# Moving two scale operations of a tile from VectorE to ScalarE, and the second tile's statistics ahead of the first tile's

## The reference

```python
# part 1: a selective scan over l for 512 channels and 16 states, added through a tanh gate
u, dt, B, C = ...            # from ctx: projection, causal conv, silu, small projections
for l in range(512):
    state = state * exp(dt[l] * A) + (dt[l] * u[l]) * B[l]
    y[l] = (state * C[l]).sum(-1)
y = (y + D * u) * silu(layernorm(x))
x = x + tanh(g_xattn) * y.T
# part 2: a gated MLP with weights of -1, 0, 1 and activations rounded to 8 bit
def bitlinear(v, w):         # v: rows of 512 (gate, up) or 2048 (down)
    v = v * rsqrt(mean(v*v) + 1e-6)
    s = 127 / clip(max|v|, 1e-5)
    return round(clip(v*s, -128, 127)) / s  @  (round(clip(w*sw, -1, 1)) / sw).T
n = layernorm(x)
h = silu(bitlinear(n, w_gate)) * bitlinear(n, w_up)
x = x + tanh(g_ffn) * bitlinear(h, w_down)
```

## Time and profile before

| | us |
|---|---|
| median of 3 runs | 628.78 |
| lowest, highest | 627.72, 630.99 |
| profiled execution, own time | 626.36 |
| its span in the trace | 624.5 |
| mean granted TensorE clock of the profiled run, share of full speed | 0.969 |

### The profile page before, as it was taken

The page is one execution under the profiler, slowest core; times in us unless marked ns, Lnnn a source line. Parts: engine busy times, 40 slices in busy tenths (PEclk is TensorE's granted clock), DMA queues, the critical chain, the costliest instruction groups (busy, mean ns, idle before and its releaser), DMA issues. The chain is left out here.

```text
span 624.5 us, 9211 instructions
## 1 busy us (share of the span) xinstructions
PE 502.3 (80%) x3014; PEld 337.1 (54%) x3014; DVE 564.4 (90%) x777; ACT 511.4 (82%) x761; POOL 519.6 (83%) x286
## 2 busy tenths in 40 slices
PE   6999665866676788879777888888687978799997
PEld 2443354755574565656454655555455655555553
DVE  2899989999999999999998999999989999987564
ACT  4869799886997898969598989786889898778784
POOL 2568799999999999999999999999999999941000
PEclk9999768889889999999999999999999999999999
DMA  8992931710840010018301101075101110000001
GB/s 282 399 413 92 363 127 34 270 51 2 312 188 6 11 41 5 31 35 334 143 30 35 35 34 35 35 268 204 35 34 35 35 34 19 1 17 18 18 18 50
DMA packets 29985, 64.47 MB, mean 103 GB/s; under 512 B 3681, under 2 KB 11873, under 8 KB 26866
## 3 DMA queue, kind: packets, MB, share of 16 engines
q1 hardware_dynamic: 29938, 63.89, 28.2%
HBM read 55.75 MB, written 8.13 MB: 102 GB/s over the span
## 5 line engine op out<-in xcount | busy, mean ns | idle before, releaser
L755 POOL TENSOR_TENSOR area_s<-area_s,b_bc 128x1024 f32<-128x1024 f32 x128 | 300.7, 2368 | 10.0 <-DVE u_all L1318 5.7
L438 PE MATMUL pY<-ident,area_s 128*128 128x128 f32 x640 | 103.1, 287 | 79.2 <-DVE area_s L1326 76.3
L438 PEld LDWEIGHTS pY<-ident,area_s 128*128 128x128 f32 x640 | 73.2, 145 | 107.5 <-DVE area_s L1326 78.4
L1002 ACT ACTIVATE pA<-dt_all,a_neg 128x512 f32<-128x512 f32 x160 | 107.8, 682 | 19.2 <-DVE area_s L1318 13.8
L1318 DVE TENSOR_TENSOR_SCAN area_s<-pA,area_s 128x512 f32<-128x512 f32 x96 | 114.3, 1205 | 4.8 <-ACT pA L1002 4.8
L481 PE MATMUL pG<-wq_gu,area_f 128*128 128x512 fp8e4 x448 | 106.1, 379 | 4.9 <-ACT area_f L952 3.6
L747 POOL TENSOR_TENSOR u_all<-u_all 128x1024 f32<-128x1024 f32 x44 | 104.1, 2366 | 0.2 <-DMA u_all<-bc_rows 0.2
L1326 DVE TENSOR_TENSOR area_s<-area_s,pC 128x512 f32<-128x512 f32 x144 | 95.3, 664 | 1.6 <-DVE area_s L1318 0.9
L432 PE MATMUL pC<-ident,xdT 128*128 128x128 f32 x576 | 90.5, 284 | 3.8 <-DVE area_s L1326 2.6
L432 PEld LDWEIGHTS pC<-ident,xdT 128*128 128x128 f32 x576 | 69.6, 143 | 11.5 <-DVE area_s L1326 9.2
L481 PEld LDWEIGHTS pG<-wq_gu,area_f 128*128 128x128 bf16 x448 | 41.1, 98 | 52.3 <-ACT area_f L960 5.2
(11 more groups left out here) (197 smaller groups left out, 978.2 us busy)
## 6 DMA issues: line engine op xcount, KB each, us to landing
b_bc<-bc_rows SPq DMA_DIRECT2D x16, 1024.0 KB, 7.4
area_s<-x SPq DMA_DIRECT2D x32, 256.0 KB, 3.0
u_all<-bc_rows SPq DMA_DIRECT2D x14, 512.0 KB, 6.0
b_bc<-w_gate SPq DMA_DIRECT2D x1, 4096.0 KB, 15.2
...
```

The lines of the kernel that those rows point to most:

```text
L438: mm = pe.matmul(pY[:, k * P:(k + 1) * P], src[:, k * P:(k + 1) * P], ident[:, :], is_transpose=True, start=(first and k == 0), stop=(last ...
L755: gp.tensor_tensor(db[c % NDB], du[s % 2].rearrange("p (a l) -> p a l", a=1).to_broadcast([P, CH, L]), b_bc[:, CH * c:CH * c + CH, :], ALU ...
L1002: act.activation(exp_bank(s, n), dt_all[:, s, :], ACT.Exp, scale=a_neg[:, s % NT, n:n + 1]).then_inc(S["s_exp"], 1)
```

## The change

Five edits.

1. CS leaves `x_scales`: ScalarE computes it in `gate_scale`, right after `scale_x` (in the late part after `copy_xqT`). The semaphore f_xs now counts four per tile and CS has f_cs.
2. OSC leaves `h_scales`: ScalarE computes it in `out_scale`, after the second `scale_h` (before the `copy_hqT`s). f_hs now counts three per tile and OSC has f_osc.
3. In a first-tile step VectorE's `x_scales(t1)` moves from n = 7 to n = 6 (ahead of scan 7 and the product of state 6), GpSimd's `x_rstd(t1)` one `times_b` forward, ScalarE's `scale_x(t1)` from n = 8 to n = 7.
4. In a first-tile step ScalarE's `x_sum`, `centre` (n = 3) and `x_deviation` (n = 4) of the second tile move ahead of `centre` of the first one, to where they are in the other steps; the variance is now an operation of its own (`x_variance`), at n = 7 in a first-tile step.
5. `centre(t1)` stands ahead of `scale_h`, not behind it, at n = 5; `x_scales` of a unit's first tile waits for both centrings, since they count on one semaphore, and the squares of a unit's second tile go to its own buffer.

The core of the diff:

```diff
@@ GpSimd, step
                 times_b(s, NDB + 1)
-                times_b(s, NDB + 2)

                 if t1 % NT == 0:
                     x_rstd(t1)
+                times_b(s, NDB + 2)
@@ ScalarE
             def x_sum(t):

                 act.wait_ge(S["s_x1"], (t // NT) * NT + NT)
-                act.wait_ge(S["f_xn"], t)
+
+                past(act, S["f_xn"], t - (1 if (t - 1) % NT == 0 else 0))
                 past(act, S["f_xqp"], t - 1)
...
+            def gate_scale(t):
+                act.wait_ge(S["f_xs"], 4 * t + 2)
+                past(act, S["f_silu"], FC * t - FC)
+                act.activation(col(CS[t % 2]), col(M2), ACT.Copy, scale=k_gate[:, :]).then_inc(S["f_cs"], 1)
...
+            def out_scale(t):
+                act.wait_ge(S["f_hs"], 3 * t + 1)
+                past(act, S["f_o"], t - 1)
+                act.activation(col(OSC[t % 2]), col(M3), ACT.Copy, scale=k_out[:, :]).then_inc(S["f_osc"], 1)
@@ ScalarE, step
-                    if n == (2 if t1 % NT else 8):
+                    if n == (2 if t1 % NT else 7):
                         scale_x(t1)
-                    if n == 3 and t1 % NT and (t1 + 1) % NT:
+                        gate_scale(t1)
+                    if n == 3 and (t1 + 1) % NT:
                         x_sum(t1 + 1)
                         centre(t1 + 1)
-                    if n == 4 and t1 % NT and (t1 + 1) % NT:
+                    if n == 4 and (t1 + 1) % NT:
                         x_deviation(t1 + 1)
+                        if t1 % NT:
+                            x_variance(t1 + 1)
+                    if n == 5 and t1 % NT == 0:
+                        centre(t1)
                     if n == (4 if t1 % NT else 9):
                         copy_xqT(t1, pG[0][:, :])
                     if n in (5, 6) and t2 >= 0:
                         scale_h(t2, n - 5)
-                    if n == 5 and t1 % NT == 0:
-                        centre(t1)
+                        if n == 6:
+                            out_scale(t2)
+                    if n == 7 and t1 % NT == 0:
+                        x_variance(t1 + 1)
...
-                    if n == 9 and t1 % NT == 0:
-                        x_sum(t1 + 1)
-                    if n == 10 and t1 % NT == 0:
-                        centre(t1 + 1)
-                        x_deviation(t1 + 1)
@@ ScalarE, late part
                 scale_h(t - 1, 1)
+                out_scale(t - 1)
                 copy_hqT(t - 1, 0, pC_banks)
                 copy_hqT(t - 1, 1, pC_banks)
                 scale_x(t + 1)
                 gate_silu(t, 3, late_bank(3, 0))
                 copy_xqT(t + 1, pY[:, :])
+                gate_scale(t + 1)
@@ VectorE
             def x_scales(t):
                 m2 = col(M2)
-                dve.wait_ge(S["f_xn"], t + 1)
+
+                dve.wait_ge(S["f_xn"], t + (2 if t % NT == 0 and t < UNITS - NT else 1))
+                past(dve, S["f_cs"], t)
...
-                dve.tensor_scalar(col(CS[t % 2]), m2, k_gate[:, :], None, ALU.mult).then_inc(S["f_xs"], 1)
...
-                dve.tensor_scalar(col(OSC[t % 2]), col(M3), k_out[:, :], None, ALU.mult).then_inc(S["f_hs"], 1)
@@ VectorE, step
-                    if n == 7 and t1 % NT == 0:
+                    if n == 6 and t1 % NT == 0:
                         x_scales(t1)
```

42 lines of the change are left out of this document (21 added, 21 removed).

## The result

| | before | changed |
|---|---|---|
| median of 20 runs each, us | 628.13 (627.08 to 630.99) | 630.92 (629.08 to 635.09) |
| profiled execution, us (span) | 626.36 (624.5) | 631.82 (630.0) |
| ratio of the medians, 95% interval | | 1.0046 (1.0034 to 1.0059) |

The changed kernel is 2.8 us slower. That is inside my range (626.0 to 631.9) and just under the 0.5% that I called no change, but the interval leaves no doubt that it is slower, and the loss is nearly three times the 1.0 us that I had worked out. The two profiled executions lie 5.5 us apart, twice as far as the medians, so a part of what their rows show is one execution's own; the experiments had to separate it.

What follows compares the result with a forecast made beforehand. GpSimd bounds ordinary main-stage steps, VectorE only around first-tile steps. Profiled 626.36 us -0.55 + 2 x 0.6 - 0.12 + 0.57 - 0.12 = +1.0, 627.4; with the median 2.4 above the profile, 629.8 us, range 626.0 to 631.9.

Steps and rivals of the forecast that it cites:

- The bound: Main stage, ordinary steps: GpSimd sets the pace; edits leaving its work alone can win at most 4.4 us there.
- rival A: VectorE sets the pace throughout, so all work taken from it counts: 3.5 us faster, 625.3 us; chance 12%.
- Steps 8 and 12: First-tile steps: ScalarE's sum waits for GpSimd's residual, copy_xqT comes 1.0 us later; 0.6 us lost in each.
- gate 2: Steps 8 and 12, TensorE: moves by 1.0 less its 0.26 us wait for the first silu, 0.7 us later.
- The next step: Step behind a first-tile step: line 1295's small operation, gone from VectorE, gives 0.12 us back.
- Step 4: First-tile step without second-half tile: product of state 10 starts 0.44 us earlier; 0.55 us won with step 5.
- the wait for the root: Step 4, VectorE: the first tile's 0.36 us wait goes, less a remaining 0.04 us gap.
- Late part: From 561 us: TensorE waits for scale_x, now behind out_scale; 0.19 us more in each of three tiles, 0.57 us.
- closing chain: End of the kernel: line 1295's small operation leaves VectorE, 0.12 us won.
- Rival C: Steps 8, 12: TensorE's hqT transposes make xq transposes late; a step loses 1.6 us, not 0.6; 631.8 us; 15%.
- All of it moves by 1.0: Steps 8 and 12: TensorE's gates 0, 1, pooled sum, broadcast and VectorE's state-10 product shift with copy_xqT, 1.0 us later.

Runs made afterwards that it cites:

- pool_more: Kernel before plus one unread one-column product on GpSimd in steps 6, 7, 10, 11 and 14; 629.39 us, ratio 1.0017.
- small: Kernel before with only the two small products (gates' and output's scale) moved from VectorE to ScalarE, order unchanged; 629.69 us, ratio 1.0012.
- fill_after: Changed kernel plus groups of zero transposes, changing no value, in TensorE's idle time of steps 4, 8 and 12; 628.87 us, ratio 1.0004.
- fill_before: Kernel before plus groups of zero transposes in its own TensorE gaps of steps 4, 8 and 12; 627.53 us, ratio 0.9991.
- order: Changed kernel with its new order, but both small products back on VectorE; 627.55 us, ratio 1.0005.
- small_late: The run small, but in the late part ScalarE's output scale stands behind scale_x of the next tile; 629.00 us, ratio 1.0008.
- ahead: Changed kernel with TensorE's y_sum(6) and state 7's broadcast of C ahead of hqT transposes 2 and 3 in first-tile steps; 628.34 us, ratio 1.0004.
- the second comparison: Changed kernel run once more, unchanged, beside the kernel before; 630.84 us, ratio 1.0040.
- place7: Changed kernel with the first tile's root, x_scales and scale_x put back, second tile's passes in their new place; 629.28 us, ratio 1.0017.
- warm4: Changed kernel plus 24 unread transposes on TensorE in step 4, ahead of y_sum for state 6; 629.81 us, ratio 1.0019.

## Why the prediction was right, and where not

**The bound: right.** GpSimd sets the pace of ordinary steps. pool_more shows it, and so do steps 6 and 7, 10 and 11, which kept 30.9 us with 32 operations gone from VectorE. Nor does small, which has the small products moved and none of the order's costs, gain anything there (steps 6, 7, 10 and 11: 30.95, 30.91, 30.94 and 30.92), where rival A had a gain in each. The Trainium skill (Perfetto Trace Analysis, Identifying the Most-Contended Engine) would have the engine of highest occupancy relieved first. On VectorE, 89 to 90% busy, that won nothing in these steps.

**Steps 8 and 12: mechanism right at full clock.** ScalarE's sum stood blocked until the residual, copy_xqT came 1.02 us later (16.81 us behind the step's gated product, before 15.79), gate 2 came 0.60 us later (22.44 us behind it, before 21.84) where I had 0.7, and the step grew by 0.58. The next step gave back 0.25 rather than 0.12 us, but the one behind it took 0.11 of that again: the gated product of an ordinary step stands behind GpSimd, so VectorE's smaller load only moved the boundary between the two.

**Step 4: right at full clock.** Steps 4 and 5 together were 0.74 us shorter in fill_after than in fill_before, 0.67 with step 6; I had 0.55. Of the 0.44 for step 4 itself, which came out at 0.56, order shows the parts: with line 1270's product back on VectorE the step still won 0.43, where the wait for the root alone had been priced at 0.32.

**Late part: right.** 0.59 us for the three tiles (small against small_late), where I had 0.57. For the closing chain's 0.12 there is no sign: the end part of small_late is 0.06 longer than that of the kernel before, not shorter.

**The hit is in part luck.** The changed kernel lost 2.8 us where I had 1.0. The forecast of 629.8 is only 1.1 us below the 630.92 because it started from the median of three executions, 628.78, which lay 0.65 above that of twenty. Rival C, at 631.8, came nearer.

**The step that failed** is one that the prediction took without a word: "All of it moves by 1.0". It moved TensorE's work in time and left each operation its length. I had the warning at hand, and named it in rival C as a lateness: the hqT copies come later. I asked only whether the transposes would then be late, not what TensorE's longer stand before them does. It is this: at 2.14 us of idle time there, both steps fell to 0.50 of the clock in every profile that I have (6 of 6), and each fall cost 1.2 to 1.6 us (36.96 to 37.37 against 35.72). Where the clock fell, the path is rival C's: copy_xqT waits for TensorE's transposes, and the step loses 2 us. But C had them late at full clock, and that is refuted: in fill_after copy_xqT doesn't wait, and in ahead, where TensorE's work is moved out of the way of the xq transposes, the step at full clock is only 0.08 us shorter.

**Does it add up?** Not to the end. At full clock the loss is 0.8 us, and two falls of 1.5 us in steps 8 and 12 make it 3.8; measured are 2.8, and 2.4 in the second comparison. Two things could make up the 1 us. The stretch ahead of step 4, in which both kernels execute the same instructions, took 180.90 and 180.43 us in the changed kernel's two profiles and 181.18 and 181.96 in those of the kernel before, 0.9 less on average. But place7, order and ahead have the same instructions there too, and took 182.40, 182.37 and 181.90, and over all 14 profiles it ranges from 180.43 to 182.94, so these 0.9 us are more likely chance. Or not every execution of the changed kernel has both falls, as the fast ones of warm4 suggest. Which it is stays open.

The Trainium skill (TensorE: Matmul & The Clock Gate, Part 1: The HAM clock gate) says that the unit which gates the clock runs free of the kernel, so that one kernel meets its changes at different points from run to run. The trace agrees for step 4, 34.13 and 31.69 us in two executions of one kernel. It doesn't explain why steps 8 and 12 of the changed kernel fell each time, nor why small fell in step 12 and not in step 8, twice; what decides between these stays open.
